# Cross attention in a decoder layer: value products of two units in one go, four units of probabilities kept

## The chip, the core and the metric

One core of a Trainium2 chip runs the whole kernel. The metric is the time of one execution in microseconds (us); three runs of the kernel before took 257.34 to 257.71 us, with a median of 257.7. Engines: TensorE (PE in the profile; its weight loads are PEld), VectorE (DVE), ScalarE (ACT), GpSimd (POOL) and SyncE (SP). Each takes its own instructions in order, and they wait for each other by semaphores.

## The reference, cut to what matters

A post-norm decoder layer: self-attention, cross attention, a mixture of experts, each followed by a layer norm. The change is in the cross attention. Batch 2, 256 queries each, 512 context rows of 64, 16 heads.

```python
    q_hk = (hidden_q @ Wq.T).reshape(b, s, H, K)
    q_big = jnp.einsum('bshk,hkq->bshq', q_hk, w_kc_q)
    kv_rope = kv_c * cos[None] + _rotate_half(kv_c) * sin[None]
    q_r = jnp.einsum('bshq,hqr->bhsr', q_big, W_qr)
    k_r = jnp.einsum('bld,hdr->bhlr', kv_rope, W_kr)
    scores = jnp.einsum('bhsr,bhlr->bhsl', q_r, k_r)
    attn = jax.nn.softmax(scores, axis=-1)
    ctx_c = jnp.einsum('bhsl,bld->bhsd', attn, kv_rope)
    ctx_lat = jnp.einsum('bhsd,hkd->bshk', ctx_c, w_kc_kv)
    out = ctx_lat.reshape(b, s, H * K) @ Wo.T
```

## The kernel before, in words

The weights of each head are folded ahead of the stage (M_sb for queries, U_sb for outputs). A unit is a pair of heads of one batch: 16 units (NUNIT), unit m with pair m % 8 of batch m // 8. A loop over n runs on every engine, and each engine writes its instructions of n in an order laid down by hand; LAG is 2, so one iteration works on several units at once.

On TensorE, iteration n has four rounds r. A round has the two score products (xmax, L808 and L809) whose row maxima are wanted for unit n, and the two score products (xexp, L835 and L836) for the exponentials of unit n-2, transposed, so that keys lie on partitions. Round 1 also transposes the maxima of unit n-1 (xmaxT, L819); it waits until VectorE has split these maxima and has written the low parts of query n+1. Round 3 also forms query n+2 (L792). At n=3 and 4 there are projections of the self-attention between rounds, at n=12, 13, 16 and 17 the output projections (out_proj, L872), at 14 to 17 parts of the router. After the rounds come the value products of unit n-3 (xpv, L858: eight products, each for 64 rows of the output, the two heads side by side) and the products of its summed probabilities with ones (xsum, L845), which give the softmax's denominators. The maxima's products alternate between two PSUM banks: product u waits until VectorE has read product u-2. Value products and denominators of unit m lie in bank 4 + m % 2 and wait for the normalization of unit m-2.

On VectorE, iteration n has the four maxima of unit n (xmax, L1425), their split into a coarse and a fine part (xmax_split: a cast L1432, a copy L1434, a subtraction), the reciprocal of the denominators of unit n-4 (xrecip, L1443) and its product with the values (xnorm, L1448), and the low parts of query n+2 (query_lo, L1418), which wait for ScalarE's high parts. At n=3, 4, 13, 14 and 15 the statistics and applications of layer norms (norm_stats, norm_apply L1356) stand between these; at n=14 an application and statistics stand between the first and the second maximum.

ScalarE takes the exponentials (L1198) into probs, which holds two units, spreads the transposed maxima (L1226) and copies the high parts of the queries (L1190). GpSimd adds a unit's four blocks of probabilities into psums, two units deep (L451, L455: three adds per unit), clears rows of QB (L412) and copies query halves (L419). The exponentials of unit m wait for value products and adds of unit m-2; the adds wait for the products with ones of unit m-2. The last unit's adds are VectorE's (L1532).

Of the kernel before, what the change touches and what calls it, by code (L numbers as in the profile page):

```python
# [22 lines left out]
ACT = mybir.ActivationFunctionType  # L23
ALU = mybir.AluOpType
AX = mybir.AxisListType

P = 128
# [3 lines left out]
SEQ = 256  # L31
# [6 lines left out]
NKC = LK // P  # L38
# [3 lines left out]
NUNIT = 2 * NPAIR  # L42
# [19 lines left out]
LAG = 2  # L62
# [6 lines left out]
def decoder_layer(nc, xT_in, pk_in, rope_in, spread_in, wE_in, wcT_in, wq_in, bv_up, xn_in, bo, wop_in, wu_in, sh_in,  # L69
                  kv_in, w13_in, w2_in, out):  # L70
    stack = ExitStack()
    with stack:
        def sb(name, shape, dt=F32, scope=stack):
            return scope.enter_context(nc.sbuf_tensor(name, shape, dt))
# [12 lines left out]
        probs = sb("probs", [P, 2, NKC, 512])  # L87
# [69 lines left out]
        late = ExitStack()  # L157
# [23 lines left out]
        xmneg = sb("xmneg", [P, 4, 2, 2], scope=late)  # L181
        xmhi = sb("xmhi", [P, 4, 2, 2], F32R, scope=late)
        xmsplit = sb("xmsplit", [P, 4, 2, 2, 2], scope=late)
        psums = sb("psums", [P, 2, 512], scope=late)
        xrcp = sb("xrcp", [P, 2, SEQ], scope=late)
        late.close()

        ps = stack.enter_context(nc.psum_tensor("ps", [P, 8, 512], F32))
# [106 lines left out]
        stored = sem("stored")  # L295

        block = stack.enter_context(nc.Block())

# [36 lines left out]
        def _(pool):  # L337
# [105 lines left out]
            for n in range(NUNIT + LAG - 1):  # L443

                m = n - LAG
                if m >= 0:
                    s = m % 2
                    pool.wait_ge(xexp_sb, NKC * m + 2)
                    if m >= 2:
                        pool.wait_ge(xsum_done, m - 1)  # L450
                    g.tensor_tensor(psums[:, s, :], probs[:, s, 0, :], probs[:, s, 1, :], ALU.add).then_inc(xadd_sb, 1)  # L451
                    for kc in range(2, NKC):
                        pool.wait_ge(xexp_sb, NKC * m + kc + 1)
                        pool.wait_ge(xadd_sb, 3 * m + kc - 1)
                        g.tensor_tensor(psums[:, s, :], psums[:, s, :], probs[:, s, kc, :], ALU.add).then_inc(xadd_sb, 1)  # L455
                if n + 2 < NUNIT:
                    if m >= 0:
                        pool.wait_ge(xadd_sb, 3 * m + 3)
                    else:
                        pool.wait_ge(const2, 2)  # L460
                    blank_maxima(n + 2)
                    other_half(n + 2)
                if n in (3, 4):
                    reciprocal_root(0, n - 1)
                if n == NPAIR + LAG + 3:
                    reciprocal_root(1, 0)
                if n == NPAIR + LAG + 4:
                    reciprocal_root(1, 1)
# [34 lines left out]
        def _(pe):  # L503
# [334 lines left out]
            def xsum(n):  # L838

                if n == NUNIT - 1:  # L840
                    pe.wait_ge(xlast_sb, NKC - 1)
                else:
                    pe.wait_ge(xadd_sb, 3 * n + 3)
                for hh in range(2):
                    mm = pe.matmul(ps[DC * hh:DC * hh + DC, 4 + n % 2, SEQ:2 * SEQ], ones64[:],  # L845
                                   psums[:, n % 2, hh * SEQ:(hh + 1) * SEQ], start=True, stop=True)
                mm.then_inc(xsum_done, 1)

            def xpv(n, kc):

                b = n // NPAIR
                pe.wait_ge(xexp_sb, NKC * n + kc + 1)
                if kc == 0 and n < 2:
                    pe.wait_ge(sums_sb, NGRP)
                if kc == 0 and n >= 2:
                    pe.wait_ge(ctxn_sb, n - 1)
                for hh in range(2):
                    mm = pe.matmul(ps[DC * hh:DC * hh + DC, 4 + n % 2, 0:SEQ], kv_dup[:, NKC * b + kc, 0, :],  # L858
                                   probs[:, n % 2, kc, hh * SEQ:(hh + 1) * SEQ], start=(kc == 0), stop=(kc == NKC - 1))
                if kc == NKC - 1:  # L860
                    mm.then_inc(xpv_done, 1)

# [93 lines left out]
            for n in range(NUNIT + LAG):  # L956
                for r in range(4):

                    if n == 0 and r % 2 == 0:
                        attn_exp(NGRP - 1, r // 2)  # L960
                    if n < 3 and r == 0:
                        attn_sum(NGRP - 3 + n)
                    if n == 0 and r in (0, 2):
                        keep_warm(6)
                    if n < NUNIT:
                        xmax(n, r)
                    if LAG <= n < NUNIT + LAG:
                        xexp(n - LAG, r)

                    if n < 2 and r == 2:  # L970
                        attn_pv(NGRP - 2 + n)
                    if n in (3, 4) and r < 2:
                        if n == 3 and r == 0:
                            pe.wait_ge(mT_sb, NGRP)
                        if n == 4 and r == 0:
                            pe.wait_ge(r_sb[0], 3)
                        attn_proj(n - 1, ps[:, 7, 0:D], (2 * r, 2 * r + 1))
                    if n == 5 and r in (1, 3):
                        if r == 1:
# [24 lines left out]
                    if n == NUNIT + 1 and r == 1:  # L1004
                        out_proj(2, 4)
                        out_proj(3, 4)
                        spread_gates(0, 1)
                    if n == NUNIT + 1 and r == 3:
                        out_proj(2, 5)
                        out_proj(3, 5)  # L1010
                        spread_gates(0, 2)
                    if n == 1 and r == 1:
                        keep_warm(6)
                    if r == 1 and 1 <= n <= NUNIT:
                        xmaxT(n - 1)
                    if r == 3 and n + 2 < NUNIT:
                        query(n + 2)
                if n >= LAG + 1:
                    for kc in range(NKC):
                        xpv(n - LAG - 1, kc)  # L1020
                    xsum(n - LAG - 1)
            spread_gates(0, 3)
            for kc in range(NKC):
                xpv(NUNIT - 1, kc)
# [41 lines left out]
        def _(act):  # L1066
# [125 lines left out]
            def xexp(n, kc):  # L1192
                u = NKC * n + kc
                act.wait_ge(xexp_ps, u + 1)
                if kc == 0 and n >= 2:
                    act.wait_ge(xpv_done, n - 1)
                    act.wait_ge(xadd_sb, 3 * n - 3)
                a.activation(probs[:, n % 2, kc, :], ps[:, 2 + u % 2, :], ACT.Exp).then_inc(xexp_sb, 1)  # L1198

            def gate_exp(b, o):  # L1200
                act.wait_ge(gate_ps, b + 1)
# [72 lines left out]
        def _(dve):  # L1274
# [215 lines left out]
            for n in range(NUNIT + LAG + 2):  # L1490
# [12 lines left out]
                    norm_apply(0, n - 2, x1)  # L1503
                if n < NUNIT:
                    xmax(n, 1)
                if n < NUNIT:
                    xmax(n, 2)
                if n < 3:
# [3 lines left out]
                    xmax_split(n)  # L1512
                if n in (3, 4):
                    norm_stats(0, n - 1, ps[:, 7, 0:D], x_nat)
                if n >= LAG + 2:
                    xrecip(n - LAG - 2)
                    xnorm(n - LAG - 2)
                if n + 2 < NUNIT:
                    query_lo(n + 2)
                if NUNIT <= n < NUNIT + 2:  # L1520
# [2 lines left out]
                if n == NUNIT + 1:  # L1523

                    for kc in range(1, NKC):
                        dve.wait_ge(xexp_sb, NKC * (NUNIT - 1) + kc + 1)
                        if kc == 1:
                            dve.wait_ge(xsum_done, NUNIT - 2)
                        else:
                            dve.wait_ge(xlast_sb, kc - 1)  # L1530
                        s = (NUNIT - 1) % 2
                        v.tensor_tensor(psums[:, s, :], probs[:, s, 0, :] if kc == 1 else psums[:, s, :], probs[:, s, kc, :],  # L1532
                                        ALU.add).then_inc(xlast_sb, 1)

            def hidden(q):
# [140 lines left out]
```

## Time and profile before

| | us |
|---|---|
| median of three runs | 257.7 |
| profiled execution, whole | 257.63 |
| its span, first to last instruction | 255.9 |
| TensorE busy | 239.8 |
| VectorE busy | 196.0 |
| ScalarE busy | 120.5 |
| GpSimd busy | 115.9 |

The granted clock of TensorE is 0.998 of full speed over the span, at the upper level of 2.4 GHz. Rows of the timeline have start (us from the span's start), duration, engine, line, operation, output and input tiles; in brackets the idle time of that engine just before, and what ended it. Matmuls overlap: a row's duration reaches past the next one's start, so their pace is read from starts, and "x16" over 1.95 us are sixteen passes.

### The profile page before, as it was taken

Reading aid. Unit: us, or ns where it says so; the run is one execution under the profiler, and the core shown is the slowest. Engines: PE = TensorE matmul, PEld = TensorE weight load, DVE = VectorE, ACT = ScalarE, POOL = GpSimd, SP = SyncE. Lnnn points to the kernel's source line nnn. Section 1 sums busy time; section 2 is a strip of 40 time slices with the busy share of each in tenths; the row PEclk is TensorE's granted clock in tenths of the full one; section 3 lists DMA queues with packets and bytes.
Section 4 is the critical chain, followed back from the end, with each engine's and each line's share of the span. In section 5 each row is a group of like instructions: output and inputs, shape, how many; then the busy total and the mean of one; then the engine's idle time right before and its main releaser. Section 6 shows DMA issues by size and latency. Waiting matters only on the chain.

```text
span 255.9 us, 4411 instructions
## 1 busy us (share of the span) xinstructions
PE 239.8 (94%) x1581; PEld 172.9 (68%) x1581; DVE 196.0 (77%) x351; ACT 120.5 (47%) x253; POOL 115.9 (45%) x167
## 2 busy tenths in 40 slices
PE   8989999988999999998999999999999999988991
PEld 5478797754656567775676767677776777767870
DVE  1377577899865999769889999986668895886684
ACT  2555367556366355454355655434325534313450
POOL 7297400000027437856487666666375534011272
PEclk9999999999999999999999999999999999999999
DMA  6999940000000840000000000000000000000002
GB/s 241 322 289 328 412 178 3 1 1 3 0 3 1 154 95 0 0 0 0 4 0 0 4 0 0 4 0 0 3 0 0 4 0 0 3 0 0 0 3 82
DMA packets 4500, 13.66 MB, mean 53 GB/s; under 512 B 512, under 2 KB 1280, under 8 KB 4352
## 3 DMA queue, kind: packets, MB, share of 16 engines
q1 hardware_dynamic: 4048, 11.29, 13.2%
q0 software_dynamic: 432, 2.10, 3.8%
q8 instruction: 13, 0.21, 0.4%
q14 instruction: 7, 0.06, 0.1%
HBM read 14.43 MB, written 0.52 MB: 58 GB/s over the span
## 4 chain that ended last, share of the span: by engine, by line
PE 76%; DVE 18%; ACT 3%; issue 2%; POOL 0%; POOLq 0%
PE ps L858 11%; PE ps L808 6%; PE ps L835 5%; PE ps L836 5%; PE ps L809 5%; PE ps L872 5%; PE ps L792 4%; DVE rcp L1334 3%; PE ps L509 3%; PE ps L648 3%; PE ps L937 3%; DVE mneg L1363 3%; PE ps L845 3%; PE ps L695 2%; DVE xmneg L1425 2%
## 5 line engine op out<-in xcount | busy, mean ns | idle before, releaser
L1198 ACT ACTIVATE probs<-ps 128x512 f32<-128x512 f32 x64 | 38.0, 597 | 57.0 <-PE ps L836 55.9
L1425 DVE TENSOR_REDUCE xmneg<-ps 128x1 f32<-128x512 f32 x64 | 43.2, 689 | 17.9 <-PE ps L809 17.5
L455 POOL TENSOR_TENSOR psums<-psums,probs 128x512 f32<-128x512 f32 x30 | 38.7, 1289 | 10.8 <-ACT probs L1198 8.2
L451 POOL TENSOR_TENSOR psums<-probs 128x512 f32<-128x512 f32 x15 | 19.2, 1283 | 31.1 <-ACT probs L1198 19.6
L808 PE MATMUL ps<-KA,QA 128*128 128x512 f32 x64 | 30.1, 470 | 2.1 <-DVE xmneg L1425 2.1
L858 PE MATMUL ps<-probs,kv_dup 128*64 128x256 f32 x256 | 31.2, 385 | 0.0
L1443 DVE RECIPROCAL xrcp<-ps 128x256 f32<-128x256 f32 x16 | 28.0, 1752 | 2.4 <-PE ps L845 2.4
L399 POOL TENSOR_TENSOR rstd<-mv,eps_col 128x1 f32<-128x1 f32 x12 | 2.3, 188 | 59.3 <-DVE mv L1351 59.0
L1363 DVE TENSOR_REDUCE mneg<-ps 128x4 f32<-128x1024 f32 x16 | 19.6, 1224 | 9.3 <-PE ps L588 8.9
L835 PE MATMUL ps<-QA,KA 128*128 128x512 f32 x64 | 26.0, 406 | 0.0
L836 PE MATMUL ps<-QB,KB 68*128 68x512 f32 x64 | 25.4, 397 | 0.0
L809 PE MATMUL ps<-KB,QB 68*128 68x512 f32 x64 | 25.2, 394 | 0.0
L858 PEld LDWEIGHTS ps<-probs,kv_dup 128*64 128x64 f32 x256 | 17.0, 136 | 11.2 <-ACT probs L1198 3.0
L1103 ACT ACTIVATE probs<-ps 128x512 f32<-128x512 f32 x32 | 17.3, 593 | 10.6 <-PE ps L614 10.5
L808 PEld LDWEIGHTS ps<-KA,QA 128*128 128x128 f32 x64 | 12.0, 188 | 11.9 <-DVE xmneg L1425 5.9
L792 PE MATMUL ps<-x1T,M_sb 128*128 128x256 f32 x64 | 16.4, 380 | 0.5 <-ACT x1T L1148 0.5
L872 PE MATMUL ps<-U_sb,ctxn 128*128 128x256 f32 x64 | 16.5, 380 | 0.0
L1190 ACT ACTIVATE QA<-ps 64x256 fp32r<-64x256 f32 x32 | 12.1, 378 | 8.8 <-PE ps L792 8.4
L1418 DVE TENSOR_TENSOR QB<-ps,QA 64x256 fp32r<-64x256 f32 x32 | 13.3, 416 | 3.7 <-ACT QA L1190 3.2
L1226 ACT ACTIVATE QB<-ps,own_rows 4x256 fp32r<-4x256 f32 x32 | 13.1, 455 | 4.9 <-PE ps L819 4.6
L1220 ACT ACTIVATE sil<-ps 128x256 f32<-128x256 f32 x18 | 6.9, 382 | 16.5 <-PE ps L937 15.5
L835 PEld LDWEIGHTS ps<-QA,KA 128*128 128x128 f32 x64 | 12.1, 190 | 3.3 <-issue 0.8
(165 smaller groups left out, 475.1 us busy)
## 6 DMA issues: line engine op xcount, KB each, us to landing
wu<-in_wu SPq DMA_DIRECT2D x4, 640.0 KB, 8.2
wq<-in_wq SPq DMA_DIRECT2D x4, 512.0 KB, 13.1
wcT<-in_wcT SPq DMA_DIRECT2D x4, 384.0 KB, 12.1
wE<-in_wE SPq DMA_DIRECT2D x4, 320.0 KB, 11.2
w13T<-in_w POOLq DMA_DIRECT2D x1, 1024.0 KB, 7.6
x1T<-in_xT SPq DMA_DIRECT2D x1, 512.0 KB, 3.7
kvp<-in_kv POOLq DMA_DIRECT2D x1, 512.0 KB, 6.1
x_nat<-in_xn SPq DMA_DIRECT2D x1, 512.0 KB, 18.0
```

The source lines that it names most:

```text
L455: g.tensor_tensor(psums[:, s, :], psums[:, s, :], probs[:, s, kc, :], ALU.add).then_inc(xadd_sb, 1)
L792: mm = pe.matmul(ps[:, query_bank(n), 0:SEQ], M_sb[:, c, p, :], x1T[:, c, b * SEQ:(b + 1) * SEQ], start=(c == 0), stop=(c == 1))
L808: pe.matmul(o, QA[:, s, hh, q], KA[:, b * LK:(b + 1) * LK], start=True, stop=False)
L809: pe.matmul(o, QB[:, s, hh, q], KB[:, b * LK:(b + 1) * LK], start=False, stop=True).then_inc(xmax_ps, 1)
L835: pe.matmul(o, KA[:, k0:k0 + P], QA[:, s, :, :], start=True, stop=False)
L836: pe.matmul(o, KB[:, k0:k0 + P], QB[:, s, :, :], start=False, stop=True).then_inc(xexp_ps, 1)
L858: mm = pe.matmul(ps[DC * hh:DC * hh + DC, 4 + n % 2, 0:SEQ], kv_dup[:, NKC * b + kc, 0, :], probs[:, n % 2, kc, hh * SEQ:(hh + 1) * SEQ], ...
L872: mm = pe.matmul(o, ctxn[:, p, t * P:(t + 1) * P], U_sb[:, p, :], start=(p == 0 and t < 2), stop=(p == NPAIR - 1))
L1198: a.activation(probs[:, n % 2, kc, :], ps[:, 2 + u % 2, :], ACT.Exp).then_inc(xexp_sb, 1)
L1363: v.tensor_reduce(mneg[:, i % 2, :, 2 * pr:2 * pr + 2].rearrange("p u h -> p h u"), ps[:, 0:2, :].rearrange("p h (u k) -> p h u k", u=2), ...
L1425: v.tensor_reduce(xmneg[:, n % 4, qt, hh:hh + 1], ps[:, u % 2, :], AX.X, ALU.max, negate=True).then_inc(xmax_sb, 1)
L1443: v.reciprocal(xrcp[:, n % 2, :], ps[:, 4 + n % 2, SEQ:2 * SEQ]).then_inc(xrcp_sb, 1)
```

## The change

xprobs gives unit n's block of probabilities: probs for n % 4 below 2, the new probs_up above, so four units are kept, and psums is four units deep. The waits of exponentials and adds move from unit n-2 to unit n-4. value_units(n) lists the units whose value products TensorE makes at the end of iteration n: at even n from 4 to 16 units n-4 and n-3, at 17 unit 14; unit 15 comes after the loop as before. All value products of the list come first, then all products with ones. normed_units(n) lists the units that VectorE normalizes at n: n-5 from 5 to 16, units 12 and 13 at 17, then 14 and 15; reciprocal and normalization stand behind the second maximum, no longer behind the split. Two output projections at the end move one step later.

```diff
-        psums = sb("psums", [P, 2, 512], scope=late)
+        psums = sb("psums", [P, 4, 512], scope=late)
+        probs_up = sb("probs_up", [P, 2, NKC, 512], scope=late)
...
+        def xprobs(n):
+            return (probs if n % 4 < 2 else probs_up)[:, n % 2]
+        def value_units(n):
+            if n == NUNIT + 1:
+                return [NUNIT - 2]
+            return [n - LAG - 2, n - LAG - 1] if n >= LAG + 2 and n % 2 == 0 else []
+        def normed_units(n):
+            if n < NUNIT + 1:
+                return [n - LAG - 3] if n >= LAG + 3 else []
+            return [NUNIT - 4, NUNIT - 3] if n == NUNIT + 1 else [n - LAG - 2]
...
-                    if m >= 2:
-                        pool.wait_ge(xsum_done, m - 1)
+                    if m >= 4:
+                        pool.wait_ge(xsum_done, m - 3)
...
                     if n == NUNIT + 1 and r == 1:
+                        spread_gates(0, 1)
+                    if n == NUNIT + 1 and r == 3:
                         out_proj(2, 4)
                         out_proj(3, 4)
-                        spread_gates(0, 1)
-                    if n == NUNIT + 1 and r == 3:
-                        out_proj(2, 5)
-                        out_proj(3, 5)
                         spread_gates(0, 2)
...
-                if n >= LAG + 1:
+                for m in value_units(n):
                     for kc in range(NKC):
-                        xpv(n - LAG - 1, kc)
-                    xsum(n - LAG - 1)
+                        xpv(m, kc)
+                for m in value_units(n):
+                    xsum(m)
+            out_proj(2, 5)
+            out_proj(3, 5)
             spread_gates(0, 3)
...
-                if kc == 0 and n >= 2:
-                    act.wait_ge(xpv_done, n - 1)
-                    act.wait_ge(xadd_sb, 3 * n - 3)
+                if kc == 0 and n >= 4:
+                    act.wait_ge(xpv_done, n - 3)
+                    act.wait_ge(xadd_sb, 3 * n - 9)
...
                 if n < NUNIT:
                     xmax(n, 1)
+                for m in normed_units(n):
+                    xrecip(m)
+                    xnorm(m)
                 if n < NUNIT:
                     xmax(n, 2)
...
-                if n >= LAG + 2:
-                    xrecip(n - LAG - 2)
-                    xnorm(n - LAG - 2)
```

## Rows read from the trace of the kernel before

**Rows 1.** The page's first part: busy us, share of the span and instructions.

```profile
PE 239.8 (94%) x1581; PEld 172.9 (68%) x1581; DVE 196.0 (77%) x351; ACT 120.5 (47%) x253; POOL 115.9 (45%) x167
```

**Rows 2.** Waits of TensorE from 86 to 225: total us, times, longest.

```profile
PE ps L808 <- DVE xmneg L1425: 2.1, 6, 0.8
```

**Rows 3.** Timeline, TensorE: first score product for exponentials at n=3, 7, 11, 17.

```profile
98.32 0.39 PE L835 MATMUL ps<-QA,KA 128*128 128x512 f32 x1
...
133.40 0.39 PE L835 MATMUL ps<-QA,KA 128*128 128x512 f32 x1
...
163.05 0.40 PE L835 MATMUL ps<-QA,KA 128*128 128x512 f32 x1
...
215.64 0.50 PE L835 MATMUL ps<-QA,KA 128*128 128x512 f32 x1
```

**Rows 4.** Timeline, TensorE, value products of n=9 and the iteration behind them.

```profile
151.88 1.03 PE L792 MATMUL ps<-x1T,M_sb 128*128 128x256 f32 x4
...
152.84 1.95 PE L858 MATMUL ps<-probs,kv_dup 128*64 128x256 f32 x16
...
154.62 0.60 PE L845 MATMUL ps<-psums,ones 128*64 128x256 f32 x4
...
155.15 0.49 PE L808 MATMUL ps<-KA,QA 128*128 128x512 f32 x1
...
155.48 0.40 PE L809 MATMUL ps<-KB,QB 68*128 68x512 f32 x1
...
157.13 0.38 PE L819 MATMUL ps<-ident,xmsplit 128*4 128x128 f32 x2
...
157.59 0.39 PE L809 MATMUL ps<-KB,QB 68*128 68x512 f32 x1
...
158.29 0.39 PE L808 MATMUL ps<-KA,QA 128*128 128x512 f32 x1
...
158.52 0.39 PE L809 MATMUL ps<-KB,QB 68*128 68x512 f32 x1
```

**Rows 5.** Timeline, ScalarE, VectorE and GpSimd in the same iteration.

```profile
157.33 0.60 ACT L1198 ACTIVATE probs<-ps 128x512 f32<-128x512 f32 x1 [0.35 <-PE ps L836]
...
158.95 0.69 DVE L1425 TENSOR_REDUCE xmneg<-ps 128x1 f32<-128x512 f32 x1 [0.23 <-PE ps L809]
...
159.49 2.71 POOL L455 TENSOR_TENSOR psums<-psums,probs 128x512 f32<-128x512 f32 x2
159.67 1.13 DVE L1432 CAST xmhi<-xmneg 128x4 fp32r<-128x4 f32 x1
...
160.28 0.78 ACT L1190 ACTIVATE QA<-ps 64x256 fp32r<-64x256 f32 x2 [0.27 <-PE ps L792]
...
160.99 1.75 DVE L1443 RECIPROCAL xrcp<-ps 128x256 f32<-128x256 f32 x1
...
162.26 0.52 POOL L412 MEMSET QB<- 4x512 f32 x1
...
162.77 0.42 DVE L1448 TENSOR_TENSOR ctxn<-ps,xrcp 128x256 f32<-128x256 f32 x1
...
163.11 0.86 DVE L1418 TENSOR_TENSOR QB<-ps,QA 64x256 fp32r<-64x256 f32 x2
...
164.01 1.29 DVE L1425 TENSOR_REDUCE xmneg<-ps 128x1 f32<-128x512 f32 x2
```

**Rows 6.** Casts by line (min/median/max ns), then timeline at n=5, 14 and 16.

```profile
L1432 DVE CAST xmhi<-xmneg x16: 170/780/1132, 86.4 to 203.5; 128x4 fp32r<-128x4 f32 x16
...
118.93 1.38 DVE L1356 TENSOR_SCALAR x<-resid,mv,rstd 128x256 f32<-128x256 f32 x1
118.95 0.50 PE L808 MATMUL ps<-KA,QA 128*128 128x512 f32 x1 [0.30 <-DVE xmneg L1425]
...
195.09 0.19 PEld L808 LDWEIGHTS ps<-KA,QA 128*128 128x128 f32 x1 [0.69 <-DVE xmneg L1425]
...
213.44 1.28 DVE L1484 TENSOR_TENSOR xe<-x2T,ps 128x512 bf16<-128x512 f32 x2 [2.15 <-PE ps L910]
```

More of the change, by code:

```diff
@@ L446, in _ @@
                 if m >= 0:
-                    s = m % 2
+                    s = m % 4
                     pool.wait_ge(xexp_sb, NKC * m + 2)
-                    if m >= 2:
-                        pool.wait_ge(xsum_done, m - 1)
-                    g.tensor_tensor(psums[:, s, :], probs[:, s, 0, :], probs[:, s, 1, :], ALU.add).then_inc(xadd_sb, 1)
+                    if m >= 4:
+                        pool.wait_ge(xsum_done, m - 3)
+                    g.tensor_tensor(psums[:, s, :], xprobs(m)[:, 0, :], xprobs(m)[:, 1, :], ALU.add).then_inc(xadd_sb, 1)
                     for kc in range(2, NKC):
@@ L454, in _ @@
                         pool.wait_ge(xadd_sb, 3 * m + kc - 1)
-                        g.tensor_tensor(psums[:, s, :], psums[:, s, :], probs[:, s, kc, :], ALU.add).then_inc(xadd_sb, 1)
+                        g.tensor_tensor(psums[:, s, :], psums[:, s, :], xprobs(m)[:, kc, :], ALU.add).then_inc(xadd_sb, 1)
                 if n + 2 < NUNIT:
@@ L845, in xsum @@
                     mm = pe.matmul(ps[DC * hh:DC * hh + DC, 4 + n % 2, SEQ:2 * SEQ], ones64[:],
-                                   psums[:, n % 2, hh * SEQ:(hh + 1) * SEQ], start=True, stop=True)
+                                   psums[:, n % 4, hh * SEQ:(hh + 1) * SEQ], start=True, stop=True)
                 mm.then_inc(xsum_done, 1)
@@ L858, in xpv @@
                     mm = pe.matmul(ps[DC * hh:DC * hh + DC, 4 + n % 2, 0:SEQ], kv_dup[:, NKC * b + kc, 0, :],
-                                   probs[:, n % 2, kc, hh * SEQ:(hh + 1) * SEQ], start=(kc == 0), stop=(kc == NKC - 1))
+                                   xprobs(n)[:, kc, hh * SEQ:(hh + 1) * SEQ], start=(kc == 0), stop=(kc == NKC - 1))
                 if kc == NKC - 1:
@@ L1194, in xexp @@
                 act.wait_ge(xexp_ps, u + 1)
-                if kc == 0 and n >= 2:
-                    act.wait_ge(xpv_done, n - 1)
-                    act.wait_ge(xadd_sb, 3 * n - 3)
-                a.activation(probs[:, n % 2, kc, :], ps[:, 2 + u % 2, :], ACT.Exp).then_inc(xexp_sb, 1)
+                if kc == 0 and n >= 4:
+                    act.wait_ge(xpv_done, n - 3)
+                    act.wait_ge(xadd_sb, 3 * n - 9)
+                a.activation(xprobs(n)[:, kc, :], ps[:, 2 + u % 2, :], ACT.Exp).then_inc(xexp_sb, 1)
             def gate_exp(b, o):
@@ L1527, in _ @@
                         if kc == 1:
-                            dve.wait_ge(xsum_done, NUNIT - 2)
+                            dve.wait_ge(xsum_done, NUNIT - 4)
                         else:
                             dve.wait_ge(xlast_sb, kc - 1)
-                        s = (NUNIT - 1) % 2
-                        v.tensor_tensor(psums[:, s, :], probs[:, s, 0, :] if kc == 1 else psums[:, s, :], probs[:, s, kc, :],
+                        s, last = (NUNIT - 1) % 4, xprobs(NUNIT - 1)
+                        v.tensor_tensor(psums[:, s, :], last[:, 0, :] if kc == 1 else psums[:, s, :], last[:, kc, :],
                                         ALU.add).then_inc(xlast_sb, 1)
```

## Prediction

> **What bounds the kernel now.** I read the page's engine shares first: TensorE is busy for 94% of the span and VectorE for 77% [rows 1], which says that one waits for the other rarely, but not where. So next the waits of TensorE over the cross attention: 2.1 us in six waits, all for the row maxima [rows 2]. Then the timeline, for where an iteration n of the unit loop begins (the first score product of exponentials, L835): n=3 at 98.32, n=7 at 133.40, n=11 at 163.05, n=17 at 215.64 [rows 3]. Four plain iterations, 7 to 10, take 29.65 us, 7.41 each.
>
> One such iteration piece by piece [rows 4], by starts, since ends of matmuls are modelled. Score products start 0.23 apart (158.29, 158.52), so a pair (L808+L809 or L835+L836) costs 0.465; eight pairs 3.72. The maxima's transposes take 0.23 (L819 at 157.13; L809 at 157.59 less one product). The query's four passes take 0.87 (the last starts 0.65 into the 1.03 of L792, so 0.217 each). Sixteen passes of value products take 1.78 (152.84 to 154.62), 0.111 each; with the four passes of products with ones 2.23. Sum 7.05. The rest is lost at both ends of that group, the only one with 64-column weights here: the query ends by its passes at 152.75 and the group starts at 152.84; it ends at 155.07, L808 loads and starts at 155.15, and L809 follows 0.33 later, not 0.23. Together 0.09 + 0.08 + 0.10 = 0.27 per group. Floor of an iteration: 7.32.
>
> VectorE in the same iteration [rows 5]: four maxima (0.69 alone, 0.60 apart when back to back), split (cast, copy, subtract), reciprocal 1.78 to the next start, normalization 0.34, low query parts 0.90: 2.4 + 0.37 + 2.12 + 0.90 = 5.8 without waits. But the split's cast, 0.17 at its shortest, has a median of 0.78 [rows 6]. The one at 159.67 lasts 1.13: it starts inside the first of two adds of GpSimd (159.49, 2.71 for both with a gap of 0.15) and ends at 160.80, as that add does [rows 5]. I call this a hold. So VectorE needs 5.8 to 6.9 of 7.4: spread evenly, it keeps up.
>
> **The change part by part.** *Grouping.* The groups of 64-column products go from 16 to 9; 7 x 0.27 = 1.9 us of TensorE time goes. The products themselves stay. In exchange the iterations alternate: an odd one has no value products, 3.72 + 0.23 + 0.87 = 4.82; an even one has two units of them, 4.82 + 4.45 + 0.27 = 9.54. A pair sums to 14.36, against 14.82 now.
>
> *Reciprocals amid the maxima.* Nothing is added, but every odd iteration still asks VectorE for one whole unit, 5.8 us, within 4.82 of TensorE. It can't begin early, as the first maximum comes from that iteration's first product, and TensorE can't run ahead, as there are two banks for the maxima, the transposes of n wait at n+1 for split and low parts of n, and its instructions go in order. Odd iteration, t=0 at its first product: maxima from 0.67 (0.465 and 0.20 to VectorE's start, as 158.52 to 158.95) and from 1.60; reciprocal 2.20, normalization 3.98, third maximum 4.35, fourth 4.95 to 5.55, split to 5.92, low parts to 6.82 (the query's high parts, 0.20 + 0.78 behind its end, are there at 5.84). TensorE: ready for the next iteration at 4.82, but its first bank is read out at 5.08, and a waiting product pays 0.10 for its weights: the even iteration starts at 5.18. Its transposes come 1.86 later, 7.04. Its first maximum waits for the low parts: 6.82 to 7.42, seen at 7.55; the third product of maxima, due at 7.27, starts at 7.55 plus 0.10. From there nothing holds TensorE: 1.86 + 0.87 + 4.45 + 0.27 after 7.65 makes 15.10. VectorE is done by 14 and idles.
>
> Now the hold. GpSimd's first add of an odd iteration waits for the second exponential (0.60 each [rows 5]), at 2.7; the three adds fill 2.7 to 4.0, 4.1 to 5.4, 5.5 to 6.8. The cast falls due at 5.55, on the start of the third add; it or the copy behind it ends with that add, 1.1 late. Low parts, transposes and maximum all move by it: 16.2. I bound this hold by 0 (the shortest cast [rows 6]) and by 1.6 (the add and the clearing of QB behind it, 0.52 [rows 5]), and take 1.1: the nearest row is the cast of 1.13, met by the same add at the same place.
>
> The Trainium skill, "SBUF — State Buffer", section "SBUF: two separate sides", states that VectorE and GpSimd share a port pair as an exclusive lock, held for a whole instruction, so that the later one fully blocks. By that rule the hold of 1.1 is sure whenever the two meet, and the total is the +3.3 below; by the shortest cast it would be the +0.9 of the first rival. The rows show the end of the hold, not its cause.
>
> *Four units of probabilities.* Exponentials and adds wait for the unit four back, not two. ScalarE waits for scores, never for these, in the rows of before; worth nothing alone, needed by the grouping. The waits of GpSimd move with it, to sums done two iterations earlier.
>
> **The sum, by stretches.** (1) n=3 to 6: 35.08 now. Two groups fewer, -0.5. At n=5 the layer norm's apply sits behind the maxima and is held by an add (1.38 for some 0.4), and two products of TensorE wait behind it, 0.30 [rows 6] and the longest of the stage, 0.8 [rows 2], each with its load of 0.10: -1.3. With no normalization and low parts in front, the apply now comes at t=1.3, before GpSimd's first add. New: 0.5 at n=4 (same apply ahead of the second maximum), 0.55 at n=6, as above without hold. -0.8. (2) n=7 to 10: two pairs at 16.2 for 29.65: +2.7. (3) n=11 and 12: the start of 12 waits 0.36, but the output projections between its maxima (8 products of two passes, 8 x 0.43 = 3.5 us) cover the rest, -0.27 and -0.2 of old waits: -0.1. (4) n=13 and 14: projections in 13 cover its VectorE work, but its low parts now end 2.0 after its query (0.20 + 0.78 + 0.04 + 0.90) with no value products over them, so n=14 begins with transposes and maximum late (0.56), and the apply and statistics that stand ahead of its second maximum end later: the fourth product, which waits 0.69 for its load now [rows 6], waits about 1.1 more, by the later low parts (1.3) less what of the apply's own wait was there. With -0.27: +1.35. (5) n=15 and 16: -0.05. (6) From n=17: units 12 and 13 are normalized back to back, 4.3 us, where one was; VectorE was idle for 2.15 us ahead of its gate products [rows 6], and TensorE has the same work there. +0.2. Total -0.8 + 2.7 - 0.1 + 1.35 - 0.05 + 0.2 = +3.3 us. The profiled execution took 257.63, 0.07 under the median of three: 260.9.
>
> **Rivals.** *The hold is missed* (0.22). If the cast gets in front of the add and the copy too, a pair costs 15.10 to 15.2 instead of 16.2: +0.9, 258.5. For: the cast falls due within 0.1 us of the add's start. Against: half of the casts last 0.78 and more now [rows 6], so cast and adds meet as a rule.
> *TensorE is never held* (0.12), the side other than mine: the pair takes its floor. For: now only 2.1 us of waits [rows 2], and the reciprocal no longer stands between the fourth maximum and the next first one. It then saves 1.9 of switches and some 2.2 of waits: 253.5. It decides at an odd VectorE unit of about 5.2 us, which 2.4 + 0.37 + 2.12 + 0.90 doesn't reach; a part of it, with the hold missed and a switch worth 0.37 (were the passes 0.107), gives about no change.
> *The hold is paid twice* (0.16): cast behind the third add, copy behind the clearing, 0.5 more in each odd iteration from 5 on, or the 0.27 per group is no switch cost and stays (7 x 0.27): 262.6 to 262.8.
> *The sum as above* has 0.50.
>
> **How the numbers follow.** Forecast 260.9. The range of 257.0 to 263.0 takes in the rivals on the slow side and the missed hold with room below, and leaves out most of the 0.12 and the far end of the last. A measurement of this kernel tells changes over 0.2% (0.5 us) from none. Faster 0.12 (TensorE never held); same 0.08 (the missed hold with a dearer switch); slower 0.80.
>
> **What would show it.** In the changed profile, odd iterations (L835 to L835) of 5.2 us and even ones of 10 to 11 from n=7 on; waits of TensorE for maxima and for low query parts grown from 2.1 us to about 6 to 8, most at the transposes of odd units; VectorE idle for 2 us and more under the double value products. Cast or copy of odd units at 1.1 to 1.3 us shows the hold; both at 0.17 the first rival. The switch is right if the first L808 behind value products still shows 0.33 to its L809, 9 times or fewer. Wrong is the forecast if a pair takes under 14.8, or if the start (n=3 to 6) or the tail moves by over 1 us.

## The result, and the profile after

The changed kernel takes 267.14 us (median of four, 266.44 to 268.54) against 257.7: a ratio of 1.0365, 95% interval 1.0339 to 1.0391. That is slower, as forecast, but by more than twice as much: +9.4 us by the medians, where +3.3 was forecast and the range ended at 263.0. The profiled execution took 266.44 with a span of 264.6, against 257.63 and 255.9: +8.7 in the span, and this is the sum that has to be explained. Some executions run longer at a lower granted clock, and the ratios leave out those more than 1.5% above the fastest of their kernel (among them 268.71 of the kernel before and 400.56 with the applies behind), while medians count all.

The page's first part after the change, the answer to [rows 1]:

```profile
PE 241.3 (91%) x1581; PEld 173.5 (66%) x1581; DVE 196.6 (74%) x351; ACT 120.6 (46%) x253; POOL 115.9 (44%) x167
```

The engines have the same instructions and, TensorE apart, nearly the same busy time; shares fall because the span grew. So time was lost in waits. TensorE's waits from 86 to 235 us, the answer to [rows 2] (total us, times, longest):

```profile
PE ps L824 <- DVE xmneg L1442: 5.1, 9, 2.0
PE ps L835 <- issue: 2.4, 4, 0.8
PE ps L888 <- DVE ctxn L1465: 1.1, 1, 1.1
```

Before, the same view had 0.3 at the transposes ("issue") beside the 2.1 for maxima. So 2.4 us became 8.6, and one wait of 2.0 us is new. The starts of iterations 3, 7, 11 and 17 (L851 is L835 of before, [rows 3]):

```profile
98.37 0.39 PE L851 MATMUL ps<-QA,KA 128*128 128x512 f32 x1
...
134.29 0.39 PE L851 MATMUL ps<-QA,KA 128*128 128x512 f32 x1
...
166.53 0.39 PE L851 MATMUL ps<-QA,KA 128*128 128x512 f32 x1
...
224.06 0.50 PE L851 MATMUL ps<-QA,KA 128*128 128x512 f32 x1
```

From such starts come the stretches of the forecast, in us, each the difference of two starts. The runs below are read in the same way, because the product has a line of its own in every kernel.

| kernel | n=3 to 6 | 7 to 10 | 11, 12 | 13, 14 | 15, 16 | sum |
|---|---|---|---|---|---|---|
| before | 35.08 | 29.65 | 18.29 | 17.97 | 16.33 | 117.32 |
| forecast for after | 34.28 | 32.35 | 18.19 | 19.32 | 16.28 | 120.42 |
| after | 35.92 | 32.24 | 18.18 | 21.66 | 17.69 | 125.69 |
| after, applies behind | 34.68 | 32.25 | 18.19 | 18.62 | 18.54 | 122.28 |
| after, busy wait | 35.87 | 32.21 | 18.18 | 20.05 | 17.71 | 124.02 |
| after, short adds | 33.61 | 30.59 | 18.18 | 18.94 | 16.33 | 117.65 |
| before, short adds | 33.55 | 29.42 | 18.14 | 17.97 | 16.30 | 115.38 |
| before, amid only | 33.41 | 29.42 | 18.14 | 17.97 | 16.31 | 115.25 |
| norms in even iterations | 33.61 | 30.05 | 17.80 | 18.19 | 19.24 | 118.89 |
| the same, short adds | 33.44 | 30.03 | 17.81 | 17.78 | 16.99 | 116.05 |

The rest is small: +0.05 ahead of n=3, and from n=17 to the end 40.54 instead of 40.26. Of the +8.7, the plain iterations (7 to 12) hold +2.5, as forecast; +0.8, +3.7 and +1.4 lie in the three stretches that also have the layer norms and the routing, where +0.5 in all was forecast.

A plain pair first (7 and 8), all engines, from the end of the odd iteration on. Columns: start, duration, engine, line, operation, and in brackets the wait and who ended it:

```profile
138.06 2.72 POOL L471 TENSOR_TENSOR psums<-psums,probs 128x512 f32<-128x512 f32 x2
...
139.51 0.39 PE L851 MATMUL ps<-QA,KA 128*128 128x512 f32 x1
139.66 1.15 DVE L1451 COPY xmsplit<-xmhi 128x4 f32<-128x4 f32 x1
...
140.79 0.87 DVE L1435 TENSOR_TENSOR QB<-ps,QA 64x256 fp32r<-64x256 f32 x2
...
141.76 0.38 PE L835 MATMUL ps<-ident,xmsplit 128*4 128x128 f32 x2 [0.68 <-issue]
...
142.44 0.49 PE L824 MATMUL ps<-KA,QA 128*128 128x512 f32 x1 [0.30 <-DVE xmneg L1442]
...
145.38 3.67 PE L874 MATMUL ps<-probs,kv_dup 128*64 128x256 f32 x32
...
149.85 0.51 PE L824 MATMUL ps<-KA,QA 128*128 128x512 f32 x1
150.19 0.40 PE L825 MATMUL ps<-KB,QB 68*128 68x512 f32 x1
...
150.63 0.69 DVE L1442 TENSOR_REDUCE xmneg<-ps 128x1 f32<-128x512 f32 x1 [2.51 <-PE ps L825]
```

This is the forecast's picture. The odd unit's copy starts inside the third add and ends as that add does, at 140.8; low parts follow, and the transposes start 0.10 behind them, 0.68 late (the profile names no releaser and says "issue"). One more maximum waits 0.30. VectorE then idles 2.51 us under the double value products. The first score product behind them is 0.34 ahead of its partner (149.85 to 150.19), the switch cost at one place per pair.

Now n=14, where the new 2.0 us wait is:

```profile
195.18 0.49 PE L824 MATMUL ps<-KA,QA 128*128 128x512 f32 x1 [0.30 <-DVE xmneg L1442]
...
195.29 1.29 POOL L467 TENSOR_TENSOR psums<-probs 128x512 f32<-128x512 f32 x1
...
195.36 1.37 DVE L1373 TENSOR_SCALAR x<-resid,mv,rstd 128x256 f32<-128x256 f32 x1 [0.23 <-POOL rstd L417]
...
197.10 0.43 DVE L1366 BATCH_NORM_STATS2 stats<-resid 128x6 f32<-128x256 f32 x1
...
197.66 0.66 DVE L1442 TENSOR_REDUCE xmneg<-ps 128x1 f32<-128x512 f32 x1
...
198.37 0.50 PE L824 MATMUL ps<-KA,QA 128*128 128x512 f32 x1 [1.99 <-DVE xmneg L1442]
...
200.23 4.78 PE L874 MATMUL ps<-probs_up,kv_dup 128*64 128x256 f32 x32
```

The apply (L1373) waits for GpSimd's rstd, starts 0.07 after an add has begun and ends with it: 1.37, where the same apply took 0.41 before the change. There it began 0.92 after its iteration (192.11), and the product behind it waited 0.25:

```profile
193.03 0.41 DVE L1356 TENSOR_SCALAR x<-resid,mv,rstd 128x256 f32<-128x256 f32 x1
...
195.09 0.50 PE L808 MATMUL ps<-KA,QA 128*128 128x512 f32 x1 [0.25 <-DVE xmneg L1425]
```

In the changed kernel statistics and the second maximum stand behind the long apply, and TensorE behind that. Then the value products take 4.78 us where the pair above takes 3.67. The view by windows says why; its columns are the stretch, its length, each engine's busy share, and after POOL's the granted clock:

```profile
198.00:199.00 1.00, 0.63 (x3) 0.54 (x4) 1.00 (x2) 0.00 (x0) 0.36 (x1) 1.00 0.00 0
199.00:200.00 1.00, 1.00 (x5) 0.59 (x3) 0.98 (x1) 0.09 (x1) 0.00 (x0) 0.54 0.00 0
...
201.00:202.00 1.00, 1.00 (x8) 0.48 (x6) 0.93 (x5) 0.00 (x0) 1.00 (x2) 0.50 0.00 0
202.00:203.00 1.00, 1.00 (x10) 0.67 (x8) 0.14 (x2) 0.00 (x0) 0.55 (x1) 0.75 0.00 0
```

TensorE's clock is at the lower of its levels (0.50, 1.2 GHz) from 199 to 202.5, right behind the wait.

At n=4 the other apply ahead of a second maximum meets an add in the same way:

```profile
108.80 1.27 POOL L467 TENSOR_TENSOR psums<-probs_up 128x512 f32<-128x512 f32 x1
...
108.85 1.37 DVE L1373 TENSOR_SCALAR x<-resid,mv,rstd 128x256 f32<-128x256 f32 x1 [1.11 <-POOL rstd L417]
...
110.87 0.51 PE L824 MATMUL ps<-KA,QA 128*128 128x512 f32 x1 [1.15 <-DVE xmneg L1442]
```

And at n=16 adds meet two operations of the routing, which took 0.17 each before the change; a reciprocal, a normalization and an output projection follow them:

```profile
211.88 1.25 DVE L1476 TENSOR_SCALAR gsc<-gexp 128x16 f32<-128x16 f32 x1
...
214.78 1.31 POOL L467 TENSOR_TENSOR psums<-probs_up 128x512 f32<-128x512 f32 x1 [1.67 <-ACT probs_up L1215]
...
214.98 1.14 DVE L1495 TENSOR_TENSOR ghl<-gsc,ghl 128x16 fp32r<-128x16 f32 x1
...
216.04 1.74 DVE L1460 RECIPROCAL xrcp<-ps 128x256 f32<-128x256 f32 x1
...
218.30 1.13 PE L888 MATMUL ps<-U_sb,ctxn 128*128 128x256 f32 x4 [1.12 <-DVE ctxn L1465]
```

### The profile page after: what moved, and what is told of

Its sections match the earlier page's. It is cut to its first block, busy times and chain, and to the rows that moved or that the text cites. A ratio compares the mean times of both kernels' runs of the same rounds, so it can differ in the third digit from the quotient of the medians.

```text
span 264.6 us, 4407 instructions
## 1 busy us (share of the span) xinstructions
PE 241.3 (91%) x1581; PEld 173.5 (66%) x1581; DVE 196.6 (74%) x351; ACT 120.6 (46%) x253; POOL 115.9 (44%) x167
## 2 busy tenths in 40 slices
DMA packets 4500, 13.66 MB, mean 52 GB/s; under 512 B 512, under 2 KB 1280, under 8 KB 4352
## 4 chain that ended last, share of the span: by engine, by line
PE 57%; DVE 26%; DMA 5%; issue 4%; POOL 3%; ACT 2%; SPq 2%; POOLq 0%
PE ps L874 11%; DVE xmneg L1442 5%; DMA wq<-in_wq 5%; PE ps L824 4%; DVE xrcp L1460 4%; PE ps L888 4%; PE ps L808 3%; DVE rcp L1351 3%; PE ps L825 3%; PE ps L851 3%; PE ps L852 3%; PE ps L861 3%; PE ps L953 3%; DVE mneg L1380 3%; PE ps L664 2%
## 5 line engine op out<-in xcount | busy, mean ns | idle before, releaser
L1442 DVE TENSOR_REDUCE xmneg<-ps 128x1 f32<-128x512 f32 x64 | 42.2, 684 | 22.6 <-PE ps L825 22.3
L1215 ACT ACTIVATE probs_up<-ps 128x512 f32<-128x512 f32 x32 | 18.9, 597 | 35.4 <-PE ps L852 34.7
L1215 ACT ACTIVATE probs<-ps 128x512 f32<-128x512 f32 x32 | 19.1, 598 | 27.9 <-PE ps L852 27.6
L851 PE MATMUL ps<-QA,KA 128*128 128x512 f32 x64 | 26.2, 410 | 0.0
L471 POOL TENSOR_TENSOR psums<-psums,probs 128x512 f32<-128x512 f32 x16 | 20.7, 1294 | 7.4 <-ACT probs L1215 6.1
L1120 ACT ACTIVATE probs<-ps 128x512 f32<-128x512 f32 x32 | 17.3, 593 | 10.6 <-PE ps L630 10.5
L471 POOL TENSOR_TENSOR psums<-psums,probs_up 128x512 f32<-128x512 f32 x14 | 17.8, 1274 | 7.2 <-ACT probs_up L1215 6.5
L467 POOL TENSOR_TENSOR psums<-probs 128x512 f32<-128x512 f32 x8 | 10.3, 1284 | 16.4 <-issue 8.4
L874 PE MATMUL ps<-probs_up,kv_dup 128*64 128x256 f32 x128 | 16.0, 404 | 0.0
L467 POOL TENSOR_TENSOR psums<-probs_up 128x512 f32<-128x512 f32 x7 | 9.0, 1286 | 15.7 <-issue 9.8
```

The costliest lines, as they stand in the source:

```text
L471: g.tensor_tensor(psums[:, s, :], psums[:, s, :], xprobs(m)[:, kc, :], ALU.add).then_inc(xadd_sb, 1)
L851: pe.matmul(o, KA[:, k0:k0 + P], QA[:, s, :, :], start=True, stop=False)
L1215: a.activation(xprobs(n)[:, kc, :], ps[:, 2 + u % 2, :], ACT.Exp).then_inc(xexp_sb, 1)
L1442: v.tensor_reduce(xmneg[:, n % 4, qt, hh:hh + 1], ps[:, u % 2, :], AX.X, ALU.max, negate=True).then_inc(xmax_sb, 1)
```

## The experiments

The theory: grouping makes odd iterations short for VectorE and the query's path; most of the loss is VectorE held by GpSimd's adds in new places, and one such hold also brings the clock down. Rivals: the four units of probabilities move the adds; the grouping costs nearly all by itself; the clock fell for another reason. Runs were timed beside the kernel before, which took 257.78, 257.94 and 258.65 us (medians) in the three sets.

**Grouping alone.** The changed kernel with reciprocals and normalizations behind the split, as before.

```diff
-                for m in normed_units(n):
-                    xrecip(m)
-                    xnorm(m)
                 if n < NUNIT:
                     xmax(n, 2)
...
+                for m in normed_units(n):
+                    xrecip(m)
+                    xnorm(m)
                 if n + 2 < NUNIT:
                     query_lo(n + 2)
```

> The changed kernel with reciprocal and normalization put back behind the split of the maxima (grouping and four units of probabilities stay). Theory (an odd iteration asks VectorE for a whole unit within 4.8 us of TensorE, and the transposes of the next iteration wait for split and low query parts): with 2.1 us of reciprocal and normalization ahead of the low parts, these come later still, a pair of plain iterations takes 17 to 18.5 us instead of 16.1, and the time is 272 to 278 us. Rival (the reciprocals amid the maxima are what costs, by delaying the third and fourth maximum): a pair takes 14.4 to 14.8 and the time is 255 to 258 us.

Measured: 279.79 us in one execution at a mean granted clock of 0.98, and 284.72 to 286.65 in three at 0.94 to 0.95; the profiled one is of these three (285.09). Its waits of TensorE from 86 to 260 us:

```profile
PE ps L835 <- issue: 6.3, 6, 1.9
PE ps L824 <- DVE xmneg L1442: 5.2, 10, 1.8
```

With the reciprocal back in the path to the transposes, the two plain pairs of the profiled execution take 20.1 and 18.7 us, with TensorE at its lower level for 6.8 and 3.4 us of them. An estimate: if half of that time was lost, some 17 us are left for each, the lower end of the 17 to 18.5 expected. So the move amid the maxima is what makes the grouping bearable: without it the shortest execution is still 12.7 us over the 267.1. The times are beyond the expected 272 to 278; how much of the excess is clock was not separated by a run.

**Amid alone.** The kernel before with only the move.

```diff
                 if n < NUNIT:
                     xmax(n, 1)
+                if n >= LAG + 2:
+                    xrecip(n - LAG - 2)
+                    xnorm(n - LAG - 2)
...
-                if n >= LAG + 2:
-                    xrecip(n - LAG - 2)
-                    xnorm(n - LAG - 2)
```

> The kernel before with only the move of reciprocal and normalization between the second and third maximum (unit n-4, no grouping, two units of probabilities). Theory: the move takes 2.1 us out of the chain from fourth maximum to transposes; the waits at n=5 and the small ones in plain iterations go, and the time falls by 1 to 2.5 us, to 255.2 to 256.7 us; plain iterations take 7.3 us. Rival: the move delays the third and fourth maximum and TensorE waits for their banks: 258 to 262 us.

Measured: 256.41 us, ratio 0.9938 (0.9911 to 0.9964). From n=3 to 17 it takes 2.07 us less than before; 1.67 of it lies in n=3 to 6, and plain iterations take 7.35 to 7.36. This part of the change is a gain, and the kernel beats both others.

```profile
PE ps L808 <- DVE xmneg L1425: 1.0, 4, 0.3
```

**Applies behind the second maximum.** The changed kernel, with `norm_apply` and `norm_stats` of n=4, 5, 14 and 15 moved.

```diff
                 if n < NUNIT:
                     xmax(n, 0)
+                if n < NUNIT:
+                    xmax(n, 1)
                 if n == NPAIR + LAG + 4:
                     norm_apply(1, 0, x2)
...
-                if n < NUNIT:
-                    xmax(n, 1)
```

TensorE also waits for both applies (`r_sb[1]`) ahead of the first transposes of normed rows.

> The changed kernel with the layer norm's apply and statistics at n=4, 5, 14 and 15 moved behind the second maximum of their iteration (ahead of the reciprocal). Theory (the apply ahead of the second maximum, held by a GpSimd add, is what TensorE waits for at n=4 and n=14, and the wait at n=14 lets the clock fall to its lower level): the waits of 1.15 and 1.99 us go, the clock stays up at 199 to 203, and the time is 3.5 to 5 us shorter than the changed kernel's 266.4, 261.5 to 263. Rival (the two waits come from the lag that the grouping leaves and only move to the next instruction): 265 to 267 us.

Measured: 264.1 us, ratio 1.0229 (1.0195 to 1.0262); 1.1 over the upper end of the expected 261.5 to 263. From n=3 to 17 it takes 3.41 less than the changed kernel. Iteration 4 takes 11.42 instead of 12.85 and 14 takes 10.36 instead of 13.39, with the clock at 1.00 throughout 193 to 202. But n=15 and 16 take 0.85 more: the normed rows are late for their transposes, and the routing still meets the adds (1.25 and 1.24). The long waits for maxima are gone; two lines of the view:

```profile
PE ps L824 <- DVE xmneg L1443: 2.1, 8, 0.3
...
PE ps L672 <- DVE x L1374: 0.7, 1, 0.7
```

**Short adds in the changed kernel.** The tile of sums is set to 1 once, and each add covers 8 columns, so most of each denominator is left out.

```diff
-                    g.tensor_tensor(psums[:, s, :], xprobs(m)[:, 0, :], xprobs(m)[:, 1, :], ALU.add).then_inc(xadd_sb, 1)
+                    g.tensor_tensor(psums[:, s, 0:8], xprobs(m)[:, 0, 0:8], xprobs(m)[:, 1, 0:8], ALU.add).then_inc(xadd_sb, 1)
```

> The changed kernel with the GpSimd adds of probabilities cut to 8 of their 512 columns for units 0 to 14, after psums was set to 1 once (the denominators leave out most of the probabilities). Theory (casts, copies and applies of VectorE are held by these adds): copies of odd units and applies fall to 0.2 and 0.4 us, a pair of plain iterations takes 15.1 us instead of 16.1, and the time is 257 to 260 us. Rival (the loss is the imbalance of odd and even iterations alone, the holds lie beside it): a pair stays at 15.8 to 16.1 and the time at 264 to 266 us.

Measured: 258.61 us, ratio 1.0052 (1.0017 to 1.0088); a pair takes 15.29, and no clock falls from n=3 to 17. From n=3 to 17 it takes 8.04 less than the changed kernel (the 1.6 of the fallen clock, shown by the busy wait below, are in that).

The largest wait is still that of n=14, now with an apply of 0.44 ahead of it:

```profile
PE ps L826 <- DVE xmneg L1444: 2.8, 8, 0.9
...
193.76 0.50 PE L826 MATMUL ps<-KA,QA 128*128 128x512 f32 x1 [0.88 <-DVE xmneg L1444]
```

**Short adds in the kernel before.** The same edit, as the partner.

> The kernel before, with GpSimd's three adds cut to 8 of their 512 columns for units 0 to 14 (most of each denominator is left out of the computation; the tile of sums holds ones elsewhere). It is the partner of the run of the changed kernel with the same cut, which took 258.6 us. Theory (most of what the change costs is VectorE held by those adds, and the grouping alone costs the imbalance of odd and even iterations): the kernel before is held too, but gains less from the cut: its iteration n=5 loses 1.7 us of hold, its plain iterations go from 7.41 to about 7.32, total about 255.5 us; the grouping without holds would then cost 258.6 - 255.5 = about 3 us, and of the +9 us measured some 6 would be holds. Rival (the adds matter to both kernels alike, and the grouping itself costs nearly all): this kernel falls by as much as the changed one did (267.1 to 258.6), to about 249 to 251 us.

Measured: 256.21 us, ratio 0.9929 (0.9906 to 0.9952). From n=3 to 17 it takes 115.38, or 1.94 less than before (the clock dips of its profiled execution lie ahead of n=3). The rival, a fall like the changed kernel's, is out. So without the long adds the change as a whole costs 117.65 - 115.38 = 2.3 us, and with them 125.69 - 117.32 = 8.4: 6.1 us of the loss came through the adds. Short adds also bring GpSimd's other work forward (rstd, the clearing of QB), and the two runs don't divide the 6.1 between VectorE held and that.

**Busy wait.** 18 bf16 products that nobody reads fill the 2.0 us wait of n=14 in the changed kernel.

```diff
+                    if n == NE + 6 and r == 3:
+                        pe.wait_ge(ctxn_sb, 9)
+                        ones = ident[:].bitcast(BF16)
+                        for _ in range(18):
+                            pe.matmul(ps[:, 4, 0:2 * P], ones[:, 0:P], ones, start=True, stop=True)
                     if n < NUNIT:
                         xmax(n, r)
```

> The changed kernel with 18 bf16 products of 256 columns, whose result nobody reads, put on TensorE ahead of the fourth product of maxima at n=14, where it waits 2.0 us for VectorE. It does the same work and waits for the same tile; only TensorE has something to do meanwhile. Theory (the granted clock at 199 to 203 us fell because TensorE stood still for 2 us): the clock stays at 1.00 there, the value products of n=14 take 3.67 us instead of 4.78, iteration 14 falls by about 1.7 us if the products fit into the wait, and the total is 264.5 to 265.5 us. Rival (the clock falls there for another reason, or the products only come on top): clock .5 to .75 again behind the wait, total 266.5 to 268.5 us.

Measured: 265.32 us, ratio 1.0277 (1.0242 to 1.0312); its four executions (264.54 to 265.91) all lie below the changed kernel's four. The filler, the held product and the value products:

```profile
197.19 2.14 PE L985 MATMUL ps<-ident 128*128 128x256 bf16 x18
199.33 0.51 PE L824 MATMUL ps<-KA,QA 128*128 128x512 f32 x1
...
200.69 3.67 PE L874 MATMUL ps<-probs_up,kv_dup 128*64 128x256 f32 x32
```

and the clock behind them, by windows of the same run:

```profile
200.00:201.00 1.00, 1.00 (x9) 0.63 (x9) 0.96 (x2) 0.42 (x1) 0.00 (x0) 1.00 0.00 0
```

The held product starts 5.39 us after its iteration, as it did without the filler (198.37 - 192.98 and 199.33 - 193.94). Nothing but TensorE's activity changed; the clock stays at 1.00 and iteration 14 takes 11.78 instead of 13.39. In this place the standing still cost 1.6 us by the clock, on top of the wait itself.

**Four units of probabilities alone**, in the kernel before.

```diff
-        psums = sb("psums", [P, 2, 512], scope=late)
+        psums = sb("psums", [P, 4, 512], scope=late)
+        probs_up = sb("probs_up", [P, 2, NKC, 512], scope=late)
...
-                if kc == 0 and n >= 2:
-                    act.wait_ge(xpv_done, n - 1)
-                    act.wait_ge(xadd_sb, 3 * n - 3)
+                if kc == 0 and n >= 4:
+                    act.wait_ge(xpv_done, n - 3)
+                    act.wait_ge(xadd_sb, 3 * n - 9)
```

> The kernel before with four units of probabilities and sums kept instead of two, and nothing else of the change. Theory (ScalarE and GpSimd never wait for a free unit in the kernel before): same time within 0.2%, 257.3 to 258.3 us, plain iterations 7.41 us. Rival (the waits of GpSimd's adds for old sums set where the adds fall, and with four units they move onto VectorE's split): plain iterations 7.6 and more, over 259 us.

Measured: 257.92 us, ratio 0.9985 (0.9955 to 1.0014), stretches 35.06, 29.67, 18.25, 17.98 and 16.28. Worth nothing, as forecast.

**Normalizations in even iterations.** On top of the applies moved behind, both reciprocals of a group run in the even iteration: one amid its maxima, one under the double value products.

```diff
-                for m in normed_units(n):
+                if 6 <= n < NUNIT and n % 2 == 0 or n == NUNIT + 1:
+                    m = n - LAG - 3 if n < NUNIT else NUNIT - 3
                     xrecip(m)
                     xnorm(m)
...
+                if n >= LAG + 2 and (n % 2 == 0 or n >= NUNIT + 2):
+                    xrecip(n - LAG - 2)
+                    xnorm(n - LAG - 2)
```

> The changed kernel with the layer norm's applies behind the second maximum (as in the run of 264.1 us), and with both reciprocals and normalizations of a group done in the even iteration, one amid its maxima and one behind its split, under the double value products; odd iterations have none. Within a group the products with values and with ones of the first unit come ahead of those of the second. Theory (an odd iteration asks VectorE for 5.8 us or more within 4.8 of TensorE; moving 2.1 us of that to the even iteration takes the imbalance away): odd iteration 4.9 to 5.2, even one 9.6 to 10, pair 14.6 to 15.1 instead of 16.1, the split's cast in odd iterations no longer on the third add; total 258 to 261 us. Rival (the hold by GpSimd's adds, not the load of VectorE, sets the pair): the cast still meets an add, pair 15.8 to 16.2, total 263 to 265 us.

Measured: 262.19 us, ratio 1.0118 (1.0078 to 1.0158); the profiled execution took 260.65, the fastest 259.49. The median lies over the theory's range and under the rival's. The pair falls from 16.1 to 15.0 although the odd unit's cast is still held (1.10 at 151.98). Shorter adds alone brought it to 15.29. So the 16.1 needs both, the reciprocal in the odd iteration and the hold. Against that, n=16 grows to 13.66, with TensorE waiting 2.0 us for the routing (L905); with short adds, in the next run, it takes 11.52. The clock does not fall behind this wait:

```profile
211.93 0.39 PE L905 MATMUL ps<-ident,ghl 128*16 128x128 f32 x2 [1.98 <-DVE ghl L1495]
...
212.00:213.00 1.00, 1.00 (x6) 0.87 (x7) 0.00 (x0) 0.56 (x2) 0.00 (x0) 1.00 0.00 0
```

**The same with short adds**, to ask whether the pair can come near its floor of 14.36.

> The kernel with both normalizations of a group in the even iteration (pair 15.0 us), and GpSimd's adds cut to 8 of 512 columns for units 0 to 14 (most of each denominator is left out of the computation). Theory (what is left over the floor of 14.36 us for a pair is VectorE held by the adds in odd iterations): odd iteration 4.82, even one 9.55 to 9.6, pair 14.4, below the 14.7 that two iterations take where value products are made unit by unit without holds; total 254 to 255 us, so that the grouping's saved switches would show only with VectorE free. Rival (the query's path and the imbalance keep the pair up): pair still 14.8 to 15.0, total 257 to 259 us.

Measured: 257.05 us, ratio 0.9947 (0.9922 to 0.9973). The pair is still 15.02, so the rival has it: with VectorE unheld and without a reciprocal in the odd iteration (4.85), the query formed at its end still comes late for the even one (10.17). One pair's turn, odd to even:

```profile
150.93 0.17 DVE L1451 CAST xmhi<-xmneg 128x4 fp32r<-128x4 f32 x1
...
151.55 0.78 ACT L1209 ACTIVATE QA<-ps 64x256 fp32r<-64x256 f32 x2 [0.27 <-PE ps L810]
...
152.37 0.87 DVE L1437 TENSOR_TENSOR QB<-ps,QA 64x256 fp32r<-64x256 f32 x2 [0.99 <-ACT QA L1209]
153.27 1.29 DVE L1444 TENSOR_REDUCE xmneg<-ps 128x1 f32<-128x512 f32 x2
...
154.02 0.49 PE L826 MATMUL ps<-KA,QA 128*128 128x512 f32 x1 [0.30 <-DVE xmneg L1444]
```

VectorE stands idle for 0.99 until ScalarE has the query's high parts, and the low parts then stand ahead of the even iteration's maxima. In the kernel before, value products lay over that path in every iteration.

**Amid and applies behind**, on the kernel before: the two moves that helped, without grouping.

> The kernel before with the reciprocal and the normalization between the second and third maximum (the run of 256.4 us), and with the layer norm's applies and statistics of n=4, 5, 14 and 15 behind the second maximum instead of ahead of it. Theory (an apply ahead of the second maximum is held by GpSimd's add and holds the fourth product of maxima): the wait at n=4 or 5 goes, 0.3 to 0.6 us, and at n=15 the transposes of the normed rows wait longer for their apply, 0.4 to 0.7 us; together about the same as that run: 256.0 to 257.0 us. Rival (as in the changed kernel, where this edit was worth 3 us): 253 to 254 us.

Measured: 256.02 us (255.85 to 256.17), ratio 0.9914 (0.9882 to 0.9946). From n=3 to 17 it takes 115.61, no less than with the first move alone (115.25), and the two times can't be told apart: what n=14 gains (6.71 instead of 7.20) n=15 pays (7.83 instead of 6.95), in the new wait of the last row.

```profile
PE ps L656 <- DVE x L1357: 0.7, 1, 0.7
```

## Why the prediction was right in sign and wrong in size

**Right.** The odd VectorE unit doesn't fit its iteration. Stretch (2) moved by +2.59 against +2.7, (3) by -0.11 against -0.1, and the tail by +0.28 against +0.2. Odd iterations take 5.22 (forecast 5.18) and even ones 10.9 (10 to 11). The copy, held to the end of the third add, shows the hold of 1.1. The three rivals of the plain pair are out: the hold was not missed, TensorE was held, and the copy was held once, by the add alone, with the switch cost at one place per pair. That 16.12 came so near to 16.2 is in part luck: without the long adds the pair takes 15.29 instead of 15.10, so they cost 0.83 and not 1.1, and the two misses nearly cancel. Four units of probabilities were worth nothing.

On what holds what, the Trainium skill, "SBUF — State Buffer", section "SBUF: two separate sides", says that a VectorE operation with two SBUF inputs, or in a mode that uses both ports, and a GpSimd operation take the shared pair in turn. The prediction's "whenever the two meet" left that condition out. The rows agree for cast, copy, apply and routing operations (1.13 to 1.37, each ending within 0.15 of an add's end). They also show which VectorE work passes an add unheld: at 197.10 statistics of 0.43, and at 197.66 a maximum of 0.66, inside an add that runs from 197.09 to 198.35.

**Wrong**: stretches (1), (4) and (5), by +1.64, +2.34 and +1.41, together 5.4 = 8.7 - 3.3. The failed step is the same in each: the hold was counted for the split of the plain pairs alone, and the other operations that an add can hold were priced at their unheld times.
- (4), "waits about 1.1 more, by the later low parts (1.3) less what of the apply's own wait was there". The apply did start late, 2.38 after its iteration against 0.92; that was seen. That this puts it on the add's start, for 0.96 more, was not: the product's wait became 1.99. And the wait's second price wasn't in the sum at all: 1.6 us of slower products, shown by the busy wait. The wait is 0.64 longer than the sum had it (1.99 less the 0.25 of before and the 1.1), and with the clock's 1.6 this makes 2.24 of the 2.34; n=14 alone falls by 3.03 once the apply is out of the way. With short adds the same wait is 0.88. So of its growth by 1.74, 1.11 came through the adds and 0.63 is the lateness, for which the sum had 1.1: that term was too large and hid part of the miss.
- (1), "0.5 at n=4". The same apply was held by the same add, and 0.5 became a wait of 1.15 in an iteration that falls by 1.43 with the apply moved. The relief of n=5 is real: with the move amid the maxima alone, n=3 to 6 takes 1.67 less than before. The other term, "0.55 at n=6, as above without hold", failed too. The copy of unit 5 was held as in the plain pairs, and the transposes were 0.80 late; with short adds iterations 5 and 6 take 15.64 instead of 16.37.

```profile
123.41 1.27 DVE L1451 COPY xmsplit<-xmhi 128x4 f32<-128x4 f32 x1
...
125.63 0.38 PE L835 MATMUL ps<-ident,xmsplit 128*4 128x128 f32 x2 [0.80 <-issue]
```

- (5), "-0.05". The routing had no term. Two of its operations were held (1.25 and 1.14 instead of 0.17), and a projection waited 1.12 for the normalization behind them. With short adds the stretch is 16.33, exactly that of before, so all of the +1.36 came through the adds.

That all three come through the adds is shown by the runs with short adds: there the stretches take 33.61, 18.94 and 16.33, none over its forecast by more than 0.05. That the apply's place is a cause in (1) and (4) is shown by the applies moved; the clock's share, by the busy wait.

The signs named for a wrong forecast didn't warn: the pair was over 14.8, and start and tail moved by 0.84 and 0.28. The waits were forecast at 6 to 8 us, most at the transposes of odd units; they are 8.6, of which 5.1 are for maxima and 2.4 at transposes.

## What to carry to other kernels

When work is moved on one engine, every short operation behind it lands elsewhere against the other engine's long ones: list all that can be held, not just the ones already held, and give each the length of what it meets (0.4 became 1.37 here). Two loops' worth of work in one iteration saves switches, but the other iteration loses the cover over its longest chain: here 0.27 per switch bought a whole VectorE unit in a short iteration and, once the reciprocal was moved out of it, an uncovered query path. Even with the long adds cut away, that lost 2.3 us and 0.7 us (117.65 and 116.05 against 115.38). Try a change's parts alone: one of these three was a gain of 0.6%, one nothing, and the grouping the loss.

## What the runs showed of the hardware that was not expected

A wait of 1.99 us of TensorE, with its products at full clock before it, was followed by some 3.5 us at 0.50 to 0.54 of the clock; the same wait filled with 2.14 us of products was not. The length of a wait doesn't decide it alone: with the normalizations in even iterations, TensorE stood still for 1.98 us at n=16, and the clock stayed at 1.00 behind that. What sets the two places apart is not shown. The waits of 1.15 and 1.12 of the changed kernel at n=4 and n=16 were not followed by longer value products (3.67 both times). The Trainium skill, "TensorE: Matmul & The Clock Gate", Part 1, says that an idle array is put to 1.2 GHz and that activity releases it; the rows agree in kind at n=14, and the wait of 1.98 shows a stop without the fall.
